# A factorized pairwise-product recommender on one NeuronCore: 160 pairs instead of 128 computed with the batch in the partitions, turns done two at a time, dense features turned along with the joined sums

## What is computed

```python
rows, cols = np.triu_indices(32, k=1)            # 496 pairs
e = jnp.stack([tbl_f[ids[:, f]] for f in 32 fields], axis=1)      # (2048, 32, 64)
p, q = e[:, rows, :], e[:, cols, :]
pij = jnp.einsum('bpe,dpe,bpd->bp', p, kernel, q)                 # (2048, 496)
z = pij @ W.T + b                                                 # (2048, 256)
h = jnp.concatenate([z, dense_ctx], axis=1)                       # (2048, 272)
h = jnp.maximum(h @ W_top1 + b_top1, 0.0)                         # (2048, 512)
h = jnp.maximum(h @ W_top2 + b_top2, 0.0)                         # (2048, 256)
y = h @ W_top3                                                    # (2048, 1)
```

## Time and profile before

| | us |
|---|---|
| three runs | 1363.39, 1359.52, 1359.11 (median 1359.52) |
| the profiled execution, its own time | 1367.28 |
| its span, first to last instruction | 1365.4 |
| around the span | 1.9 |
| mean granted PE clock | 0.831 of full |

### The profile page before, as it was taken

How to read it: one execution, slowest core, us unless ns; L and a number is a source line. 1 busy time by engine, 2 the same in 40 slices (tenths; PEclk the granted TensorE clock), 3 DMA queues, 4 the chain that set the end, 5 groups by cost and what they waited for, 6 DMA issues and landing times.

```text
span 1365.4 us, 29877 instructions
## 1 busy us (share of the span) xinstructions
PE 1075.3 (79%) x11888; PEld 350.7 (26%) x11888; DVE 615.0 (45%) x559; ACT 560.2 (41%) x4205; POOL 483.7 (35%) x517
## 2 busy tenths in 40 slices
PE   4110335779999977879999985968899999999997
PEld 2000001122334311222323320222222333333333
DVE  2000001143656622234437951334334997668990
ACT  0000000084655601024447960024425993669961
POOL 6777771544232264544442035444434000000000
PEclk9555555688998866679999995779889999999999
DMA  8111110100000010100000001000000000000000
GB/s 322 26 26 27 26 26 5 20 18 17 11 14 11 10 22 15 19 17 17 17 17 10 3 13 20 16 18 18 17 14 17 3 3 3 2 2 2 3 3 2
DMA packets 21570, 29.10 MB, mean 21 GB/s; under 512 B 11108, under 2 KB 11620, under 8 KB 20920
## 3 DMA queue, kind: packets, MB, share of 16 engines
q0 software_dynamic: 16384, 16.81, 6.3%
q1 hardware_dynamic: 3368, 8.79, 1.7%
q10 hardware_dynamic: 1680, 1.61, 0.3%
HBM read 27.17 MB, written 0.01 MB: 20 GB/s over the span
## 4 chain that ended last, share of the span: by engine, by line
PE 68%; another core or an unknown queue 14%; issue 12%; DVE 3%; ACT 2%; DMA 1%; SPq 0%; ACTq 0%; DVEq 0%
PE bilinear L580 36%; PE sums L622 16%; PE bilinear L594 8%; PE bilinear L648 6%; PE bilinear L557 2%; ACT batch_prod L444 1%; DVE prod L499 1%; DVE batch_prod L510 1%; DVE w_comb_sb L480 0%; DVE prod L494 0%; DMA b_sb<-b_top 0%; DVE prod L496 0%; PE sums L606 0%; PE bilinear L530 0%
## 5 line engine op out<-in xcount | busy, mean ns | idle before, releaser
L580 PE MATMUL bilinear<-emb_t,k_sb 64*32 64x512 f32 x6144 | 623.0, 636 | 208.9 <-issue 197.3
L499 DVE TENSOR_TENSOR prod<-bilinear,emb_t 128x1024 f32<-128x1024 f32 x352 | 419.2, 1218 | 499.3 <-remote 375.7
L444 ACT ACTIVATE batch_prod<-batch_prod 128x64 f32<-128x64 f32 x2048 | 490.1, 242 | 103.6 <-DVE batch_prod L510 98.5
L365 POOL DMA_INDIRECT emb<-table,ids_sb x384 | 362.3, 944 | 440.5 <-PE bilinear L557 329.9
L444 ACT ACTIVATION_READ_ACCUMULATOR batch_prod<-batch_prod 128x1 f32 x2048 | 386.3, 189 | 1.4 <-issue 1.3
L622 PE MATMUL sums<-prod,row_sel 64*32 64x512 f32 x2944 | 293.1, 634 | 35.0 <-issue 21.4
L580 PEld LDWEIGHTS bilinear<-emb_t,k_sb 64*32 64x32 f32 x6144 | 158.8, 111 | 575.5 <-issue 516.6
L403 ACT ACTIVATE emb_t<-bilinear 128x512 f32<-128x512 f32 x64 | 37.9, 593 | 480.5 <-PE bilinear L557 285.1
L510 DVE TENSOR_TENSOR batch_prod<-bilinear,emb_first 128x1024 f32<-128x1024 f32 x128 | 156.0, 1218 | 143.6 <-remote 112.6
L594 PE MATMUL bilinear<-k_sb,emb_t 64*32 64x512 f32 x2048 | 172.8, 622 | 2.2 <-issue 0.9
L365 POOL DMA_INDIRECT emb_first<-table,ids_sb x128 | 120.9, 945 | 126.6 <-DVE batch_prod L510 83.4
(11 more groups left out here) (25 smaller groups left out, 117.7 us busy)
## 6 DMA issues: line engine op xcount, KB each, us to landing
emb<-table,ids_sb POOLq DMA_INDIRECT x384
k_sb<-k_slots SPq DMA_DIRECT2D x2, 1088.0 KB
emb_first<-table,ids_sb POOLq DMA_INDIRECT x128
k_sb<-k_slots SPq DMA_DIRECT2D x1, 1600.0 KB
k_sb<-k_slots SPq DMA_DIRECT2D x1, 1472.0 KB
k_sb<-k_slots SPq DMA_DIRECT2D x1, 960.0 KB
k_sb<-k_slots SPq DMA_DIRECT2D x1, 896.0 KB
k_sb<-k_slots SPq DMA_DIRECT2D x1, 576.0 KB
```

The costliest lines, as they stand in the source:

```text
L365: nc.gpsimd.indirect_dma_start(fields_of(i, j, t)[:, f % 2, :], None, tables[f], bass.IndirectOffsetOnAxis(ap=ids_sb[:, start + t, f:f + 1 ...
L444: last = nc.scalar.activation(products, products, ACT.Copy, accum_out=batch_sums[:, t, half, row + f:row + f + 1])
L499: last = nc.vector.tensor_tensor(prod[:, at:at + 2, 0:n], bilinear[:, bank:bank + 2, 0:n], emb_t[:, j:j + 1, 0:n].to_broadcast([P, 2, n]), ...
L580: last = nc.tensor.matmul(bilinear[col:col + QUARTER, bank + row // EMB, 0:n], k_sb[row:row + EMB, operand, col:col + QUARTER], emb_t[row: ...
```

## The change

Rows 12 and 13 join the rows that are done with the batch in the partitions, so a chunk has 40 batch units, 88 slots and 42 quads in place of 32, 96 and 46. The sum's places in `batch_sums` are handed out row by row (`BATCHED_ROWS`) since 160 doesn't divide as before. In chunks 1 to 3 two doubles are turned in one step into both banks of a ring pair and copied out by one ACT instruction of 128x1024; chunk 0 still turns one at a time. Batch units come every 1.95 slots (2.05 in the later part of chunk 0). Reduces are put into the list one at a time and kept from the step before one in which ACT has a copy to do. The dense features stay untransposed in DRAM: SP loads a chunk's with one DMA into the last 16 columns of `batch_sums`, before the join, which turns them along; PE's waits for them in the first layer go, and the 8 DMAs for their weights become one. The start's 10 copies of folded weights (DVE, L480) become 4.

```diff
-BATCHED_ROWS_OF = range(4, 12)
+BATCHED_ROWS_OF = range(4, 14)
-FIRST_LAYER = 10
+FIRST_LAYER = 12
-TURNS_EARLY = {83: 0, 85: 1, 87: 2, 89: 3, 91: 4, 93: 5}
-TURNS = {1: 6, 4: 7, 8: 8, 12: 9, 16: 10, 20: 11, 24: 12, 28: 13, 32: 14, 36: 15}
-BATCH_FROM, BATCH_EVERY = 4, 2.5
-FIRST_BATCH_FROM, FIRST_BATCHES, THEN_FROM, THEN_EVERY = 8, 8, 16, 2.8
+TURNS_EARLY = {76: 0, 80: 2, 84: 4}
+TURNS = {2: 6, 9: 8, 17: 10, 25: 12, 33: 14}
+BATCH_FROM, BATCH_EVERY = 4, 1.95
+FIRST_BATCH_FROM, FIRST_BATCHES, THEN_FROM, THEN_EVERY = 8, 8, 16, 2.05
...
+DENSE_AT = P - DENSE
+BATCHED_ROWS = [(half, 32 * b + pos) for half in range(HALVES) for b in range(4) for pos in range(BATCHED_AT, 32)][:BATCHED]
...
 def program():
+        if i > 0 and which in TURNS:
+            behind[at].append(("turn", i, (TURNS[which], 2)))
+        if i + 1 < NCHUNKS and which in TURNS_EARLY:
+            behind[at].append(("turn", i + 1, (TURNS_EARLY[which], 2)))
...
+    def for_scalar(at):
+        return any(kind in ("turn", "layer", "join") or (kind == "sum" and (which + 1) % GROUP_QUADS == 0)
+                   for kind, i, which in behind[at])
...
-            reduces += [(at + REDUCE_LAG * (half + 1), ("reduce", i, (*which, half))) for half in range(HALVES)]
-        while reduces and reduces[0][0] <= at:
+            reduces += [(at + REDUCE_LAG, ("reduce", i, (*which, half))) for half in range(HALVES)]
+        steps += behind[at]
+        if reduces and reduces[0][0] <= at and not for_scalar(at + 1):
             steps.append(reduces.pop(0)[1])
...
@@ block.sync
-            for i in range(NCHUNKS):
-                at = CHUNKS[i][0] * P
-                sp.wait_ge(s_sums_out, (i + 1) * NSUMS)
-                for b in range(8):
-                    row = 32 * (b % 4) + SPARE_AT
-                    sp.dma_start(sums_sb[row:row + SPARE, NSUMS - HALVES + b // 4, 0:cols(i)],
-                                 dense_t[b * SPARE:(b + 1) * SPARE, at:at + cols(i)]).then_inc(s_dense, 16)
+            sp.wait_ge(s_consts, 4)
+            for i, (start, tiles) in enumerate(CHUNKS):
+                wait(sp, s_joined, i)
+                sp.dma_start(batch_sums[:, 0:tiles, HALVES - 1, DENSE_AT:],
+                             dense[start * P:(start + tiles) * P, :].rearrange("(t p) f -> p t f", p=P)).then_inc(s_dense, 16)
+                if i > 0:
+                    store(sp, i - 1)
@@ block.gpsimd
-                        pool.wait_ge(s_turned, TURN_USE[i - 1, j] + 1)
+                        pool.wait_ge(s_turned, TURN_OF[i - 1, j] + 1)
@@ turn_out (ACT)
-                nc.scalar.activation(emb_t[:, j, 0:cols(i)], bilinear[:, ring_bank("turn", i, j), 0:cols(i)],
+                nc.scalar.activation(emb_t[:, j:j + several, 0:n], bilinear[:, bank:bank + several, 0:n],
                                      ACT.Copy).then_inc(s_emb_t, 1)
@@ turn (PE)
+                for n in range(several):
+                    pe.wait_ge(*gathered(i, j + n))
+                    for t in range(CHUNKS[i][1]):
+                        last = nc.tensor.transpose(bilinear[:, bank + n, t * P:(t + 1) * P], fields_of(i, j + n, t),
+                                                   ident[:])
                 last.then_inc(s_turned, 1)
@@ join (PE)
                 pe.wait_ge(s_reduced, 2 * BATCHES_TO[i + 1])
+                pe.wait_ge(s_dense, 16 * (i + 1))
@@ layer (PE)
-                        if term == NSUMS - HALVES:
-                            pe.wait_ge(s_dense, (i + 1) * (16 * 8))
```

More of the change, by code:

```diff
@@ L181, in program @@
 def program():
+    behind = [[] for _ in range(len(ALL_UNITS) + SUM_LAG + 2)]
+    for at, (kind, i, which) in enumerate(ALL_UNITS):
+        if kind != "slot":
+            continue
+        if i > 0 and which in TURNS:
+            behind[at].append(("turn", i, (TURNS[which], 2)))
+        if i + 1 < NCHUNKS and which in TURNS_EARLY:
+            behind[at].append(("turn", i + 1, (TURNS_EARLY[which], 2)))
+        k = (which - FIRST_LAYER) // LAYER_EVERY
+        if i > 0 and (which - FIRST_LAYER) % LAYER_EVERY == 0 and 0 <= k < NOUTS:
+            behind[at].append(("layer", i - 1, k))
+        behind[at + SUM_LAG] += [("sum", i, q) for q in range(NQUADS) if last_slot_of_quad(q) == which]
+        if which == NSLOTS - 1:
+            behind[at + SUM_LAG + 1].append(("join", i, 0))
+    def for_scalar(at):
+        return any(kind in ("turn", "layer", "join") or (kind == "sum" and (which + 1) % GROUP_QUADS == 0)
+                   for kind, i, which in behind[at])
     steps = [("fold", 0, 0)]
     turned = 0
-    sums, reduces = [], []
+    reduces = []
     for at, (kind, i, which) in enumerate(ALL_UNITS):
@@ L188, in program @@
             needed = max(row_of(unit) for unit in ALL_UNITS[at:at + TURNED_BEFORE] if unit[1] == 0)
-            steps += [("turn", 0, j) for j in range(turned, needed + 1)]
+            steps += [("turn", 0, (j, 1)) for j in range(turned, needed + 1)]
             turned = max(turned, needed + 1)
         steps.append((kind, i, which))
[L192 to L204, removed]
-            reduces += [(at + REDUCE_LAG * (half + 1), ("reduce", i, (*which, half))) for half in range(HALVES)]
-        while reduces and reduces[0][0] <= at:
+        if kind == "batch":
+            reduces += [(at + REDUCE_LAG, ("reduce", i, (*which, half))) for half in range(HALVES)]
+        steps += behind[at]
+        if reduces and reduces[0][0] <= at and not for_scalar(at + 1):
             steps.append(reduces.pop(0)[1])
-        while sums and sums[0][0] <= at:
-            steps.append(sums.pop(0)[1])
-    steps += [step for at, step in reduces] + [step for at, step in sums]
+    steps += [step for _, step in reduces]
+    for late in behind[len(ALL_UNITS):]:
+        steps += late
     steps += [("layer", NCHUNKS - 1, k) for k in range(NOUTS)]
@@ L220 @@
 TURN_USE = {step[1:]: n for n, step in enumerate(step for step in PROGRAM if step[0] == "turn")}
+TURN_OF = {(i, j + n): use for (i, (j, several)), use in TURN_USE.items() for n in range(several)}
 BATCH_USE = {step[1:]: n for n, step in enumerate(step for step in PROGRAM if step[0] == "batch")}
@@ L655, in _ @@
                 elif kind == "turn":
-                    turn(i, which)
+                    turn(i, *which)
                 elif kind == "slot":
@@ L686 @@
     ids = give("ids", inputs["ids"])
[L687 removed]
+    dense = give("dense", inputs["dense_ctx"])
     k = np.asarray(inputs["L0_rec_kernel"])
```

80 lines of the change are left out of this document (35 added, 45 removed).

## The result

| | before | after |
|---|---|---|
| median of four runs, us | 1359.32 (1357.87 to 1363.39) | 1432.11 (1429.21 to 1434.48) |
| profiled execution, own time / span, us | 1367.28 / 1365.4 | 1430.6 / 1428.7 |
| mean granted PE clock | 0.831 | 0.801 |

The ratio is 1.0529 (95%: 1.0498 to 1.0561): slower by 73 us, outside the range (1344 to 1410). The sign was forecast, the size was not: +27.

The account below looks back on a forecast made before the run. It took the kernel as gathers nearly serial with the products, plus clear stretches where PE, DVE and ACT are level. Terms -13.6 + 16 - 1 + 27 + 0 - 1.5 summed to +27 us: median 1387, range 1344 to 1410.

Parts of the forecast that it names:

- four quads less a chunk: PE, L622: 168 quads remain of 184, 0.85 us each; -13.6 us, bounds -13.6 and 0.
- ACT, 8 more units a chunk: Clear stretches: ACT becomes slowest; 6 us each in chunks 1 and 2, +4 in chunk 3; +16, bounds 0 and 33.
- turns by two, bank uses: PE's turns: 64 become 40, so 24 bank uses fewer; -1 us in all.
- pairs' gather runs: Doubles 8 to 15, chunks 1 and 2: runs of 16 gathers replace 8 and 8; +27 us, upper bound +41.
- chunk ends: Gathers of 32 and 16 likely join to 48 at chunk ends; 0 us, bounds -5 and +20 each.
- dense features: Before the last layers: PE's 1.5 us wait for 8 DMAs goes; -1.5 us.
- The bound of +41: Upper bound of the cost of the pairs' gather runs, if no layer falls into a hole.
- Direction: Sign of the whole change: slower, given 0.60, against 0.12 for same and 0.28 for faster.
- the 48-gather hole: Chunk ends: 32 gathers of emb_first and 16 join to 48, costing 61 us, as much as apart.
- A: Rival, faster: a run of 16 costs no more than two of 8, buffers absorb ACT's lag; 1345 us; chance 0.28.
- C: Rival, slower still: 48 gathers freeze DVE, +20 at two chunk ends; 1427 us, or 1400 without pairs' cost; chance 0.10.
- B: Rival, no change: gather run length doesn't matter but ACT binds, 16 - 16 = 0; 1359 us; chance 0.12.

Follow-up runs that it names:

- e12: The change without its 32 further pairs (rows 4 to 11, old spacing of units), against the kernel before, holding regime: 1413.88 us, 1.0398.
- e14: The change with ACT adding up 7 of 8 fields in each batch unit, holding regime: 1394.62 us, 1.0250 of the kernel before.
- e2: The kernel before with double turns and layers after slots 12, 16 and so on, free regime: 840.61 us, 0.9867.
- e18: The kernel before with double turns, later layers and gathers of chunks 1 to 3 paced by DVE's slots, holding regime: 1168.93 us, 0.8561.
- e15: The kernel before with POOL's gathers for chunks 1 to 3 paced by DVE's slots, turns single, holding regime: 1178.84 us, 0.8652.
- e16: The change with single turns and layers at their old slots, holding regime: 1389.68 us, 1.0210 of the kernel before.
- e17: The change with layers two slots earlier (FIRST_LAYER 10), turns still double, holding regime: 1412.64 us, 1.0347 of the kernel before.
- e5: The change with ACT adding up 6 of 8 fields in each batch unit, free regime: 829.37 us, 0.9732 of the kernel before.

## Why the prediction was wrong in size

By its own steps, for the holding regime:

| step | forecast | measured |
|---|---|---|
| four quads less a chunk | -13.6 | not alone; the sums below close with it |
| ACT, 8 more units a chunk | +16 | +31 (e12 to the change is +18, taken with the forecast's -13.6 of quads in it); the last eighth of ACT's sums is 38 by e14 |
| turns by two, bank uses | -1 | about -10 (e2 free -11; e18 against e15 -10) |
| pairs' gather runs | +27 | +56 in the stretches; about +65 by e12 (54, plus the 10 and 1.5 that work against it) |
| chunk ends | 0 | 63 lost against 60 to 61 |
| dense features | -1.5 | end 1.7 shorter |
| sum | +27 | -13.6 + 31 - 10 + 65 - 1.5 = +71, measured +72 to +73 |

The last line closes by its making, since 31 and 65 are both taken from e12, and it proves no term. What stands by itself are the stretches (+56), e14 and e16.

**The step that failed most is the one on the pairs' runs**: "I let two of four still fall into a hole: 75 - 7 = 68." It priced a run of 16 at 18.8 us from rows of chunk ends. Measured are 20.2 and 21.2 a run (80.8/4, 84.7/4), with one layer of the stretch inside a run and it at 6.68 us. Two things were missed. The place of the layers (FIRST_LAYER 12) takes them out of the holes: putting them back is worth 20 to 25 us (e17), and a run then costs 18.1, near the 18.8. The prediction had itself placed the layer fifth behind the turn, beyond the three bank pairs, and still gave two of four back. And PE's granted clock is 0.51 inside the hole and 0.61 in the layer behind it, so what follows the hole is slower too; the stretches of four runs of 16 have 0.78, those of eight runs of 8 had 0.96 and 0.91. The bound of +41 given there was too low as well: it knew no price above 18.8 a run. I had read the clock, and used it nowhere.

**The second is ACT's term**: "I estimate 6 us in chunk 1 and in chunk 2 ... +4 ... Chunk 0 waits for gathers and gives ACT time." The arithmetic ahead of it was right: 3.84 us a unit, "about 10 us short". What failed is the discount for three buffers. In chunks 1 and 2 together the span grew by 70; less 56 of runs, with 6.8 of quads added back, 21 are left, over 10 each, where 6 were forecast. Chunk 3, without gathers, takes 191.4 us to its join against e12's 185.9; with 3.4 of quads added back ACT costs 8.9 there, where +4 was forecast. A reading that no run isolates: a buffer lets ACT fall behind once, but doesn't shorten the queue that PE's next group, turn or join has to wait for. Chunk 0 took 7.9 less in the holding regime, so there the forecast held. In the free regime chunk 0 isn't idle either, and the term is 34 (e5).

**The third is small**: a bank use saved is worth 0.4 to 0.5 us, not "an estimate of -1 in all" for 24. What that is made of was not isolated; ACT's copies (L403, now L418) may be part of it: 37.9 us for 64 before and 33.7 for 40 after.

**What was right.** Direction, ACT at its limit in the clear (49 of 50 forecast, 50.00 and 49.63 measured), DVE at 45 (44.68 and 46.65), the 48-gather hole, dense features. Chunk 3's join waits 0.20 us for ACT, so the wait is there, but the loss lies ahead of it, in PE's 884 records in 50 us (808 in chunk 1) where there were 944. The pairs' two halves are shown apart by e17 (displaced layers, 20 to 25 us) and e16 against it (longer runs, 19), each uncertain by up to some 10 us; the clock's share in them is read from records and was not isolated.

**The rivals.** A is out on the holding chip: a run of 16 costs 20 to 21 against 6.4 to 7.2 for 8, and the buffers absorbed little. C's mechanism (+20 at each chunk end) is absent, though the time came out beside its 1427. B's premise, that grouping is free, is false here and true in the free regime, where grouping gains 11 and the sum reads -11.3 - 13.6 - 1.5 + 34 = +8 against +11 measured. So the size of the answer belongs to the pair of kernel and regime: +5.3% holding, +1.3% free. No row of the trace before could tell me of the second regime.

## What to carry to other kernels

Before moving work to an engine whose share of the page is low, take its busy time in the stretch where it would run: ACT's 41% was 48.4 of 50 us, and 32 further units cost some 31 us. A change that groups consumers (two turns in a visit) also groups what they release; look at the queue behind the semaphore and at what fills the hole meanwhile. Where bursts of software gathers hold other engines, pace them by a consumer's semaphore: it took 13.5 to 16.5% off here. In the other regime it cost 0.1%, but there it never bound; a pace that does bind where gathers hold nobody was not run.

## What the runs showed of the hardware that I had not expected

- **The same program takes 851 or 1360 us.** All of the difference is in stretches with gathers: in the change, chunk 3 takes 191.4 us to its join and the end 30.1 in both regimes, chunk 0 takes 503.9 and 215.8. POOL's gathers take 0.94 us, 1.25 us apart, in both. What decides the regime is open: it was constant within a group of runs, and one chip number showed both.
- **It isn't DVE alone that is held.** In the kernel before, on the holding chip, a turn ends by 48.5 us, and ACT, idle, copies it 87 us later (timelines of PE and ACT):

```profile
47.43 1.09 PE L557 MATMUL bilinear<-ident,emb_first 128*128 128x128 f32 x4 [5.68 <-DMA emb_first<-table,ids_sb]
135.43 0.60 ACT L403 ACTIVATE emb_t<-bilinear 128x512 f32<-128x512 f32 x1 [96.40 <-remote]
```

In the free regime (the change, run again) the copy follows its turn at once:

```profile
48.24 0.60 ACT L418 ACTIVATE emb_t<-bilinear 128x512 f32<-128x512 f32 x1 [9.48 <-PE bilinear L569]
```

And PE, in the kernel before on the holding chip, waits for nothing that the trace knows between two matmuls of one slot:

```profile
86.41 1.01 PE L580 MATMUL bilinear<-emb_t,k_sb 64*32 64x512 f32 x1 [1.78 <-issue]
89.21 1.01 PE L580 MATMUL bilinear<-emb_t,k_sb 64*32 64x512 f32 x1 [1.79 <-issue]
```

So all three engines are late in the same stretch (DVE by the earlier trace rows), in issue and in seeing semaphores, which speaks against a port shared by DVE and POOL alone. What the common resource is, no run here isolates.
- **The price of a gather depends on its neighbours**: 0.8 to 0.9 us each in runs of 8 with a layer beside them, 1.1 (e17) to 1.3 in runs of 16 and 1.3 in the run of 48, some 0.55 where one to four come in a row.
